# A graph layer's edge routing regrouped: groups of 1,024 edges, ten slots, 26 buckets, ranks by a scan

## The reference

```
x = layernorm(x + segment_sum(x[src] * norm[:, None], dst))
gate = silu(edge_attr @ W1.T + b1) @ W2.T + b2
gate = gate + sum(emb[type[src]] * (emb[type[dst]] @ adaptW.T))
msg  = gate * x[dst] * (cutoff_weight * node_vec[dst])[:, None]
agg  = segment_sum(msg, src) / segment_sum(node_vec[dst], src)
x = layernorm(layernorm(x + agg) * gamma + beta)
```

## Time and profile before

| | us |
|---|---|
| median of three runs | 3589.17 |
| lowest, highest | 3584.2, 3595.98 |
| the profiled execution's own time | 3596.59 |
| its span | 3594.8 |
| mean granted TensorE clock, share of 2.4 GHz | 0.832 |

### The profile page before, as it was taken

One profiled execution on the slowest core, in us unless ns is written; L12 is line 12 of the kernel. 1 busy time (PEld: TensorE's weight loads), 2 busy tenths in 40 slices (PEclk: granted clock), 3 DMA queues, 4 the chain that ended last, 5 costly groups with the idle time before them and its releaser, 6 DMA issues. The chain is left out here.

```text
span 3594.8 us, 69567 instructions
## 1 busy us (share of the span) xinstructions
PE 2457.2 (68%) x24398; PEld 2030.9 (56%) x24398; DVE 2434.8 (68%) x5609; ACT 1044.9 (29%) x2117; POOL 2265.9 (63%) x2116
## 2 busy tenths in 40 slices
PE   4899256677676767767677766767776767746760
PEld 3677145556555655656555655655555655646660
DVE  7755457777676776777776776777676777746654
ACT  0000123333333333333333333333333333421110
POOL 8700477777777777777777777777777777410002
PEclk9999987888788888888887877887887888868885
DMA  8000323333333333333333333333333333318871
GB/s 312 9 0 0 80 68 97 99 99 97 99 101 97 100 101 93 95 106 95 94 106 93 97 104 94 97 100 98 96 104 94 97 104 95 87 46 325 304 271 13
DMA packets 135012, 383.77 MB, mean 107 GB/s; under 512 B 53904, under 2 KB 53904, under 8 KB 128016
## 3 DMA queue, kind: packets, MB, share of 16 engines
q0 software_dynamic: 79200, 179.69, 18.7%
q1 hardware_dynamic: 53188, 198.17, 16.2%
q10 hardware_dynamic: 2284, 1.33, 0.1%
HBM read 258.83 MB, written 120.22 MB: 105 GB/s over the span
## 5 line engine op out<-in xcount | busy, mean ns | idle before, releaser
L630 POOL DMA_INDIRECT slot<-table,gidx x1616 | 1651.0, 1022 | 517.4 <-issue 485.0
L734 PEld LDWEIGHTS route<-parts,oh_r 128*128 128x128 bf16 x9696 | 810.1, 113 | 73.2 <-ACT routed L779 28.8
L734 PE MATMUL route<-parts,oh_r 128*128 128x148 bf16 x9696 | 828.8, 255 | 33.1 <-ACT routed L779 26.3
L779 ACT ACTIVATE routed<-route 128x444 bf16<-128x444 f32 x808 | 433.4, 541 | 770.4 <-PE route L734 763.7
L639 POOL DMA_INDIRECT perm<-routed,sidx x404 | 436.7, 1081 | 225.2 <-issue 207.1
L899 DVE TENSOR_SCALAR oh_r<-iota_r,spot 128x768 bf16<-128x768 f16 x1616 | 546.7, 413 | 5.2
L701 PE MATMUL rank<-oh_b,before 128*128 128x408 bf16 x202 | 87.7, 434 | 494.6 <-DVE oh_b L860 494.6
L870 DVE TENSOR_REDUCE spot<-rank 128x8 f32<-128x408 f32 x202 | 116.9, 579 | 407.9 <-PE rank L707 407.9
L701 PEld LDWEIGHTS rank<-oh_b,before 128*128 128x128 bf16 x202 | 20.2, 100 | 609.5 <-DVE oh_b L860 607.4
L668 PE MATMUL gate<-w,hid 97*128 97x96 f32 x1616 | 238.4, 294 | 161.2 <-DVE val L984 161.2
L828 ACT ACTIVATE parts<-val 128x392 bf16<-128x392 f32 x202 | 109.5, 542 | 746.3 <-DVE val L994 746.3
(11 more groups left out here) (209 smaller groups left out, 3502.7 us busy)
## 6 DMA issues: line engine op xcount, KB each, us to landing
rows<-perm SPq DMA_DIRECT2D x51, 1554.0 KB, 8.0
oh_t<-dst_row SPq DMA_DIRECT2D x101, 512.0 KB
attr<-in_edge_attr SPq DMA_DIRECT2D x101, 320.0 KB
slot<-table,gidx POOLq DMA_INDIRECT x1616
perm<-zeros SPq DMA_DIRECT2D x51, 444.0 KB, 13.6
perm<-routed,sidx POOLq DMA_INDIRECT x404
table<-tab SPq DMA_DIRECT2D x3, 676.0 KB, 4.7
xin<-in_x SPq DMA_DIRECT2D x1, 1224.0 KB, 9.8
```

Source lines behind the costliest of these rows:

```text
L630: e.indirect_dma_start(out=slot[:, s, g, :], out_offset=None, in_=table0, in_offset=bass.IndirectOffsetOnAxis(ap=gidx[:, s, g:g + 1], axis ...
L734: mm = e.matmul(route[:, bank, RC * j:RC * (j + 1)], oh_r[:, GR * g + q, bank * R // 2 + j, :], parts[:, s % 2, GR * g + q, :], start=(q = ...
L779: e.activation(routed[:, s % 2, g, bank * ROW // 2:(bank + 1) * ROW // 2], route[:, bank, 0:ROW // 2], ACT.Copy).then_inc(rows_ok, 1)
```

## The change

A group becomes 8 columns (1,024 edges), so a tile has 2 groups. A row has 10 slots. A bucket becomes two blocks (256 nodes), so there are NB = 26 buckets of 1,024 rows (CAP), and the key stored with a message has 8 bits.

- `ranks`: one step a tile over 26 x 16 = 416 columns, three matmuls. The count across the columns of a group is made on DVE: a scan over `oh_b` writes `upto`, and PE multiplies it by `ones16`. `lowered` now holds what is taken off again.
- `route_onehots`: 16 one-hots of 10 x 128, in two groups of eight. `routes`: 160 matmuls a tile in four phases of 3, 3, 2 and 2 slots a group.
- `scatter`: 2 indirect DMAs a tile, of rows of 2,960 bytes.
- The gather's indices and the edge weights are stored to HBM in the setup (`src_pid`, `weights`) and read by SP for each tile (`edges`); L849 goes. The 49th value is put in by ACT straight from PSUM (in `put_got`); L994 goes.
- Counting: 8 matmuls of 104 columns a tile in place of 4 of 204; four more operations over 128 x 1616 behind the loop. The fills of `perm` are fewer and longer, 28 for 51.
- Summing stage: 26 reads of 1,024 rows. For each bucket two halves, each with a one-hot of 128 x 80 and 80 matmuls; ACT takes 128 off the key in the second half.

```diff
-GR = 4
+GR = 8
-R = 6
+R = 10
-CAP = 896
+CAP = 1024
+PHASES = ((0, 3), (3, 6), (6, 8), (8, 10))
...
-                            e.matmul(at, before16[:, :], mine, start=True, stop=False, skip_group_check=True)
-                            e.matmul(at, lowered[:, :], mine, start=False, stop=False, skip_group_check=True)
-                            for k in range(1, GR):
-                                e.matmul(at[:, :, :, k:GR], ones16[:, :], mine[:, :, :, 0:GR - k], start=False,
-                                         stop=False, skip_group_check=True)
...
+                        e.matmul(flat, lowered[:, :], oh_b[:, :, :], start=True, stop=False, skip_group_check=True)
+                        e.matmul(flat, ones16[:, :], upto[:, :, :], start=False, stop=False, skip_group_check=True)
+                        e.matmul(at, ident_r[0:NT, bass.ds(t, 1)].broadcast_to([NT, P]),
+                                 rstart16[0:NT, :, :].unsqueeze(3).broadcast_to([NT, NB, NG, GR]),
+                                 start=False, stop=True, skip_group_check=True).then_inc(ranked, 1)
...
+                        e.tensor_tensor_scan(upto[:, :, :].rearrange("p b q -> p (b q)"),
+                                             same_group[:, :, :].rearrange("p b q -> p (b q)"),
+                                             oh_b[:, :, :].rearrange("p b q -> p (b q)"), 0.0, ALU.mult, ALU.add
+                                             ).then_inc(ohb, 1)
...
-                                e.wait_ge(routing, 2 * (NG * (t - 1) + g + 1))
+                                e.wait_ge(routing, NPH * (NG * (t - 1) + g + 1))
...
-                        over_tiles(e, NT, U, (layer1(0), 3), (ranks(0), 3), (routes(0, 2), 4), (layer1(1), 3),
-                                   (rows_of_groups, 3), (ranks(1), 3), (routes(2, NG), 4), (pick(0), 3),
-                                   (layer2(0), 3), (pick(1), 3), (layer2(1), 3), (total, 0))
+                        over_tiles(e, NT, U, (layer1(0), 3), (ranks, 3), (routes(0), 4), (layer1(1), 3),
+                                   (rows_of_groups, 3), (routes(1), 4), (pick(0), 3), (layer2(0), 3), (pick(1), 3),
+                                   (layer2(1), 3), (total, 0))
```

More of the change, by code:

```diff
@@ L582, in build @@
             gathered = [sem(f"gathered{s}", ph) for s in range(U)]
+            index_in = [sem(f"index_in{s}", ph) for s in range(U)]
+            weight_in = [sem(f"weight_in{s}", ph) for s in range(U)]
             scattered = [sem(f"scattered{s}", ph) for s in range(2)]
@@ L618, in _ @@
                     with when(e, 1):
-                        over_tiles(e, NT, U, (load, 0), (rows, 0))
+                        over_tiles(e, NT, U, (edges, 0), (load, 3), (rows, 3))
                 @block.gpsimd
@@ new lines, in ranks @@
+                    def ranks(i, s):
+                        t = U * i + s
+                        e.wait_ge(ohb, t + 1)
+                        if since(i, s, 1):
+                            e.wait_ge(placed, t)
+                            e.wait_ge(sx, t)
+                        at = rank[:, 0:NB * G].rearrange("p (b g q) -> p b g q", g=NG, q=GR)
+                        flat = rank[:, 0:NB * G].rearrange("p (b q) -> p b q", q=G)
+                        e.matmul(flat, lowered[:, :], oh_b[:, :, :], start=True, stop=False, skip_group_check=True)
[3 more added lines that the diff above has]
+                                 start=False, stop=True, skip_group_check=True).then_inc(ranked, 1)
@@ new lines, in step @@
+                            for phase, (a, b) in enumerate(PHASES):
+                                n = NPH * (NG * t + g) + phase
+                                if since(i, s, 1) or g or phase >= 2:
+                                    e.wait_ge(rows_ok, n - 1)
+                                for j in range(a, b):
+                                    for q in range(GR):
+                                        mm = e.matmul(route[:, phase % 2, RC * (j - a):RC * (j - a + 1)],
+                                                      oh_r[:, GR * g + q, j, :], parts[:, s % 2, GR * g + q, :],
+                                                      start=(q == 0), stop=(q == GR - 1))
+                                mm.then_inc(routing, 1)
@@ L769, in silu, with put_routed @@
                         return step
-                    def put_routed(g0, g1):
+                    def put_routed(g):
                         def step(i, s):
                             t = U * i + s
-                            if g0 == 0 and since(i, s, 2):
+                            if g == 0 and since(i, s, 2):
                                 e.wait_ge(scattered[s % 2], 16 * NG * pair_of(i, s))
-                            for g in range(g0, g1):
-                                for bank in range(2):
-                                    e.wait_ge(routing, 2 * NG * t + 2 * g + bank + 1)
-                                    e.activation(routed[:, s % 2, g, bank * ROW // 2:(bank + 1) * ROW // 2],
-                                                 route[:, bank, 0:ROW // 2], ACT.Copy).then_inc(rows_ok, 1)
+                            for phase, (a, b) in enumerate(PHASES):
+                                e.wait_ge(routing, NPH * (NG * t + g) + phase + 1)
+                                e.activation(routed[:, s % 2, g, RC * a:RC * b],
+                                             route[:, phase % 2, 0:RC * (b - a)], ACT.Copy).then_inc(rows_ok, 1)
                         return step
@@ L825, in step @@
                             e.wait_ge(val_ok, n + 1)
-                            if since(i, s, 2):
-                                e.wait_ge(routing, 2 * NG * (U * i + s - 1))
-                            e.activation(parts[:, s % 2, m * HC:(m + 1) * HC, 0:MW], val[:, m], ACT.Copy
+                            e.activation(parts[:, s % 2, m * HC:(m + 1) * HC, 0:C], val[:, m], ACT.Copy
                                          ).then_inc(high, 1)
```

399 lines of the change are left out of this document (216 added, 183 removed).

## The result

The changed kernel took 3935.39 us (median of 4 runs, 3933.08 to 3936.76), the kernel before 3588.59 us on the same chip: a ratio of 1.0963, 95% interval 1.0944 to 1.0983. It is slower by 347 us; I had forecast 3841 us, slower by 252. The profiled execution has a span of 3933.6 us, 338.8 more than before (the profiled execution of before was itself 7.4 us above its median, this one is at its median).

The account below looks back on a forecast made before the run. GpSimd's queue was taken to bound the main loop before, the VectorE and PE chain after. Main loop 207, last routing 2, summing 34, count 8, setup operations 1: +252 on 3596.6, 3,849, or 3,841 in run terms; range 3,690 to 3,970.

Parts of the forecast that it names:

- the range from my own terms: Whole kernel: 3,750 to 3,930, from the scan (-43), one-hots (+70), count (+46) and a partly higher PE clock (-50).
- signs of being wrong: Main loop: wrong if a tile is under 27 us, gathers wait only for issue, or PE's clock is above 0.9.
- What bounds the kernel: Main loop before: GpSimd's queue sets it, 26.9 us a tile; a saving there pays at most 1.7 us a tile.
- The chain of a tile: Main loop after: steps through VectorE, PE and messages sum to 28.93 us, mean 29.1 a tile; loop +207 us.
- my 2,910: Main loop after: us for the 100 tiles behind the first, set against 2,703 before.
- The scan: VectorE, ahead of the ranks: 416 elements take 1.02 us, 2.06 ns each; at full rate the sum is 43 us lower.
- The summing stage: VectorE bounds it at 5.6 us a half, PE needing 80 x 66 ns = 5.3; 304.6 us in all, +34.
- Rival 3: Summing stage: PE bounds it at 86 ns a product, its clock dropped by load waits; +66 more, 3,907; chance 0.10.
- Setup: Ahead of the main loop: counting matmuls add 8 us, four new VectorE operations 1 us.
- 1, the clock through the loop: Main loop: PE keeps its higher clock throughout, chain 27.1 us, loop +10, time 3,644; chance 0.12.
- 2, the loop's mean price for the extra products: Main loop: 64 extra routing products cost 85 ns each, 1.2 us a tile, time 3,963; chance 0.12.
- 4, the queue as the bound: Main loop: GpSimd's queue stays the bound, its whole saving of 2.85 us a tile shows, time 3,349; chance 0.04.

Follow-up runs that it names:

- e8_before14: The kernel before, with 14 of the 16 gathers a tile from the seventh tile on: 3584.1 us, ratio 0.9974.
- e6_turn: The changed kernel, with twelve tiles instead of six in a turn of the main loop and of the counting loop: 3905.8 us, ratio 1.0869.
- e11_split: The changed kernel, with the summing stage's one-hots in two blocks of 40 columns and each half's sum taken one half later: 3906.7 us, ratio 1.0867.
- e9_order: The changed kernel, with oh_r in three blocks and the work of PE, ACT and VectorE around it reordered: 3527.1 us, ratio 0.9805.
- e10_all: e9_order plus shifted products for the scan, twelve tiles a loop turn, and summing one-hots in two blocks of 40 columns: 3438.1 us, ratio 0.9564.
- e12_before_turn: The kernel before, with twelve tiles instead of six in a turn of the main loop and of the counting loop: 3567.8 us, ratio 0.9921.

## Why the prediction was right or wrong

**Right in sign, in mechanism of the loss, and in the range given; 94 us short of the time.** That 3935 lies in the range is owed to rivals 2 and 3, which stretched it to 3,970; the range from my own terms ended at 3,930. The two terms that took the time past it, the jumps back and the price of a product in the summing stage, had no part in that range. One of my signs of being wrong came true as I had worded it, that the gathers still wait only for issue: I had put the wait at the wrong instruction of the queue. By its own steps:

*What bounds the kernel: wrong.* GpSimd's queue did not set the main loop. That an engine waits for nothing but issue shows that it is busy, not that the others wait for it. Queue and chain were within 0.3 us, and e8_before14 shows that the chain held the tile as well. I had allowed the saving in the queue at most 1.7 us a tile; it was worth 0.07. Since the sum was made on the chain, this did not enter the number.

*The chain of a tile: right in its steps, one term missing.* Forecast and measured in the even tile above, in us:

| | forecast | measured |
|---|---|---|
| `oh_b`, scan, start of the ranks | 1.49 | 1.60 |
| ranks | 1.14 | 1.02 |
| 80 products | 6.72 | 6.10 |
| `layer1`, group rows | 1.46 | 1.50 |
| 80 products, signal | 5.38 | 5.42 |
| eight one-hots | 3.70 | 3.70 |
| messages | 9.04 | 9.25 |
| sum | 28.93 | 28.59 |

The odd tile took 29.63, as its first 80 products took 7.11. The window's copies make `put_rows` 1.2 us later there, but the wait of 1.15 us falls away for it, so they cost nothing. The mean of the two, 29.11, is the forecast 29.1, and the mean of the first 80 products over some 45 tiles is 6.73, the forecast 6.72. What is missing is the jump back. 100 tiles (2962.7) exceed my 2,910 by 52.7 us. Of these 48 are the fourteen jumps at 3.4 us (e6_turn), and 13 come from the first six tiles, which are slower; a tile with no jump near is 29.02 us (e6_turn), which gives back 8. The kernel before has the jumps too, but its 2,703 us were measured and my 2,910 built from tiles that have none. A sum of parts was set against a measured whole. (Before, 100 tiles were 2,713.7 by `oh_b`, 10.7 more than I took, which is why the term is off by 42 and not by 53.) There was luck in it as well. I had built on 25.2 us for a tile of before, and in its loop one takes 26.5 without the jump (e8_before14). So the step from tile to tile is 2.5 us and not my 3.9; the sum for the tile after is right, though the tile that it started from is not the loop's.

*The scan: right in its price, 1.03 us for 416 elements in bf16.* With the start of 0.16 us that is 2.09 ns an element, the 2.06 of the float32 scan: bf16 gained the scan nothing, while the bf16 comparison of the same 416 elements took 0.36. The Trainium skill says that the scan runs at half throughput (DVE: opcode table, instruction layouts, handler registers and perf-mode slots, Datapath and trigger behaviour); against the plain float32 operation of the earlier trace rows the trace agrees. That it replaced PE's work one for one was not quite so: shifted products would have been 56 us cheaper.

*The summing stage: wrong in the price of a product.* I had 66 ns from the routing, where a column's elements lie side by side, and used it for columns with 160 bytes between elements. It was 80.5. So PE bounds the stage and not VectorE: 6.47 us a half for my 5.6. Rival 3 named the right engine for a wrong reason: the clock was 1.00, not lower. The Trainium skill's 81 ns for a pair of weight load and product (TensorE: Matmul & The Clock Gate, Back-to-back issue gap), which I had called contradicted, agrees with this layout's 80.5 and not with the 65 to 67 ns of the others here: e11_split brought the same 80 products to 66.6 by moving the elements closer.

*Setup: +6 for +9.* The counting loop's last product starts 6.1 us later, but its first one 2.1: the loop has 4.0 for 8. Eight matmuls of 104 columns took 1.52 us, forecast 1.55.

*The rivals.* 1, the clock through the loop: it stayed at 0.82. It rose where PE's waits for VectorE (ahead of the ranks and of `layer2`) shrank: from 7.0 us a tile in the changed kernel to 4.1 in e9_order (clock 0.90) and 3.4 in e10_all (0.94). 2, the loop's mean price for the extra products: it was 76.6 ns over both steps, under the 85 of before. 4, the queue as the bound: not in this order of work, but e9_order fills the queue, at 25.6 us a tile. I had seen no room for it, as the products cannot begin before the messages end. They needn't: the one-hots, the picks and the next messages can go on beside them, if buffers and order allow.

## What to carry to other kernels

An engine that waits only for "issue" may be one of two bounds: cut its work by itself and see whether the time moves before a change is built on it. For e9_order and e10_all that test is still to be made. When a forecast sets a chain built from single tiles against a measured loop, look at every tile position of the unrolled body, the jump back among them, and take the tiles from inside the loop. A product's price comes with the layout of its weights: take it from a row with the same distance between elements, and set it against what that layout costs the engine that writes it.

## What I had not expected of the hardware

- Each jump back of the main loop cost 3.4 to 3.6 us (8 jumps, 29 us), seen as 2.4 to 2.7 us of "issue" on VectorE and about 4 on PE (46.0 us ahead of L707 in 11 turns).
- A weight column with 160 bytes between elements made a product 80.5 ns at the full clock, with 168 bytes 75.6, and with 84 or less 65 to 67.
- VectorE's bf16 comparison of 10,240 elements went from 5.49 to 10.81 us when its second operand had one value repeated along the last dimension.
- The first 80 products after PE's idle gap took 6.10 us in one tile, at a granted clock of 0.85, and 7.11 in the next, at 0.72; the second 80 took 5.38 to the end of the last in both.
- A gather of the same table rows took 1.32 us of GpSimd's queue in e12_before_turn, 1.34 in the changed kernel and 1.42 in e9_order.
